# A twelve-stage perceiver on one core: weights, constants and first contexts loaded in the normalisation ahead of their stage

## The reference

```python
# L0x, L3x: cross attention of 16 heads, own Wq, Wk, Wv, Wo (L3x masked)
# L1x: the same with 16 heads of 64, a layer-normed context and clipped exponentials
# L2x: cross attention without weights: queries x, keys and values the context
# L0a linear attention, L1a retention, L2a softmax attention with normed heads, L3a gated recurrence
# L0f experts mixed per position, L1f routed experts (top 2 of 8), L2f one of 8 matrices per position,
# L3f SwiGLU with int8-like weights scaled by 1/127
```

## Time and profile before

| | us |
|---|---|
| median of 3 runs | 3187.68 (3183.82 to 3192.27) |
| the profiled execution | 3196.44 |
| its span | 3194.8 |
| TensorE busy | 2603.5 (81%) |
| VectorE busy | 1769.5 (55%) |
| ScalarE busy | 1363.4 (43%) |
| GpSimd busy | 563.6 (18%) |

### The profile page before, as it was taken

One profiled execution on the slowest core, in us unless ns is written; L12 is line 12 of the kernel. 1 busy time (PEld: TensorE's weight loads), 2 busy tenths in 40 slices (PEclk: granted clock), 3 DMA queues, 4 the chain that ended last, 5 costly groups with the idle time before them and its releaser, 6 DMA issues. The chain is left out here.

```text
span 3194.8 us, 84173 instructions
## 1 busy us (share of the span) xinstructions
PE 2603.5 (81%) x36049; PEld 2160.8 (68%) x36049; DVE 1769.5 (55%) x3318; ACT 1363.4 (43%) x3367; POOL 563.6 (18%) x717
## 2 busy tenths in 40 slices
PE   5999677999947999999977629928986756999868
PEld 4888454777745888888865529926764635888547
DVE  4777573566645444444345415636755855666553
ACT  3777322445522344343322214406753333666332
POOL 1111001111002211111112030043322412222000
PEclk8999898999978999999986559968987787999989
DMA  2110002110012000000000223223210001111000
GB/s 68 35 35 15 15 0 86 55 55 29 16 53 67 15 19 24 15 15 2 2 11 13 68 102 135 90 69 95 90 46 5 2 28 47 46 43 43 11 30 27
DMA packets 118713, 129.74 MB, mean 41 GB/s; under 512 B 10606, under 2 KB 109882, under 8 KB 118362
## 3 DMA queue, kind: packets, MB, share of 16 engines
q1 hardware_dynamic: 113882, 110.93, 11.2%
q0 software_dynamic: 4480, 13.64, 1.3%
...
## 5 line engine op out<-in xcount | busy, mean ns | idle before, releaser
L562 ACT ACTIVATE s_ca_probs<-s_ca_scores,s_ca_neg_max 128x256 f32<-128x256 f32 x768 | 353.2, 482 | 13.4 <-DVE s_ca_neg_max L606 10.2
L606 DVE TENSOR_REDUCE s_ca_neg_max<-s_ca_scores 128x4 f32<-128x1024 f32 x192 | 234.1, 1220 | 108.5 <-PE s_ca_scores L473 55.9
L485 PE MATMUL s_ca_probs_flipped<-identity,s_ca_probs 128*128 128x128 f32 x1536 | 212.5, 282 | 15.8 <-ACT s_ca_probs L562 9.8
L1003 DVE RECIPROCAL s_cc_inv_sums<-s_cc_sums 128x512 f32<-128x512 f32 x32 | 107.4, 3357 | 182.5 <-PE s_cc_out L871 182.5
L485 PEld LDWEIGHTS s_ca_probs_flipped<-identity,s_ca_probs 128*128 128x128 f32 x1536 | 167.2, 142 | 58.9 <-ACT s_ca_probs L562 26.6
L1665 DVE COPY s_mx_w_mixed<-s_mx_ps 128x512 f32<-128x512 f32 x256 | 163.6, 683 | 61.5 <-PE s_mx_ps L1512 45.1
L568 ACT COPY s_ca_probsT<-s_ca_probs_flipped 128x512 f32<-128x512 f32 x192 | 114.7, 597 | 173.1 <-PE s_ca_probs_flipped L485 173.1
L1620 ACT COPY s_mx_w_mixed<-s_mx_ps 128x512 f32<-128x512 f32 x256 | 137.4, 589 | 117.2 <-PE s_mx_ps L1499 97.6
L163 PE MATMUL s_ln_flip<-identity,s_ln_xn 128*128 128x128 f32 x352 | 64.3, 366 | 139.4 <-DVE s_ln_xn L145 139.2
L562 ACT ACTIVATION_READ_ACCUMULATOR s_ca_probs<-s_ca_scores,s_ca_neg_max 128x1 f32 x768 | 164.7, 214 | 0.0
L789 POOL TENSOR_TENSOR s_cc_probs_of_both<-s_cc_probsT 128x1024 f32<-128x1024 f32 x32 | 76.8, 2402 | 495.3 <-DVE s_cc_probsT L994 495.3
...
## 6 DMA issues: line engine op xcount, KB each, us to landing
...
```

Source lines behind the costliest of these rows:

```text
L485: last = nc.tensor.transpose(psT[:, 2 * a + c, :], PR[b % 2][:, 4 * n + a, c * P:(c + 1) * P], ident[:, :])
L562: last = nc.scalar.activation(PR[b % 2][:, p, :], psS[:, p // 2, (p % 2) * NKEY:(p % 2 + 1) * NKEY], ACT.Exp, bias=nmax[b % 2][:, p:p + 1] ...
L606: nc.vector.tensor_reduce(nmax[b % 2][:, 4 * n:4 * n + 4], psS[:, 2 * n:2 * n + 2, :].rearrange("p r (g k) -> p r g k", g=GR), AX_X, ALU.m ...
L1003: nc.vector.reciprocal(RD[:, :, :], psD[:, :, :]).then_inc(s_rd, 1)
```

## The change

Each block's weights become an object (`ProjectionWeights`, `CrossWeights`, `ClippedWeights`, `LinearWeights`, `GateWeights`, `PositionWeights`, `ValueWeights`, `RetentionWeights`, `HeadWeights`, `SoftmaxWeights`, `TileWeights`, `RecurrenceWeights`, `QuantisedWeights`) whose tensors and semaphores outlive the stage (`held`) and whose `load` is issued on SP in the normalisation ahead. Five have a `prepare` on POOL: splits of weights and of two contexts and zeroed values (L0x, L3x, in the query projection), splits of the four weight pieces and the normalising of the first rows (L1x, in the query projection, where DVE takes the statistics of the first rows and SP loads the pieces), the reorder (L0f, in the gate stage), zeroed and copied values (L2x, in the normalisation), and the scaling of the quantised weights (L3f, in the recurrence). The tile weights of L2f are loaded in the normalisation ahead of L2a, behind L2a's own, and the quantised weights of L3f in that ahead of L3a. `project_transposed` works in pieces of 128 weight columns and of one input chunk, with two input buffers in place of the whole input. `swiglu_quantised` does the same, is written out without a loop, and interleaves up and down. The bias matmuls of the cross attentions move behind the first key and value projections. L1f (routed experts) is not touched. The semaphores of the held objects are cleared once at the end, with one more barrier. The stages not shown below replace their loads by the object's fields.

```diff
+@contextmanager
+def held(nc, kept):
...
+        def sem(name):
+            s = nc.alloc_semaphore(unique(name))
+            kept.append(s)
+            return s
+
+        yield sb, sem
...
+class ProjectionWeights:
+
+    def __init__(self, sb, sem, w, bias, chunks):
+        self.w, self.bias = w, bias
+        self.W, self.B = sb("pj_w", [P, KC, chunks * P]), sb("pj_b", [P, chunks])
+        self.s_w, self.s_b = sem("pj_w_loaded"), sem("pj_bias_loaded")
+
+    def load(self, sp):
+        sp.dma_start(self.W[:, :, :], rows_to_sbuf(self.w)).then_inc(self.s_w, 16)
+        if self.bias is not None:
+            sp.dma_start(self.B[:, :], self.bias).then_inc(self.s_b, 16)
...
+    def prepare(self, pool):
+        for u in range(2):
+            pool.memset(self.V[u][:, :, :, :, :], 0.0).then_inc(self.s_set, 1)
+        if self.OWN:
+            pool.wait_ge(self.s_wkv, 16)
+            pool.tensor_copy(self.WH[:, :, :], self.W[:, :, :]).then_inc(self.s_wh, 1)
+            pool.wait_ge(self.s_wh, 1)
+            pool.tensor_tensor(self.WL[:, :, :], self.W[:, :, :], self.WH[:, :, :].bitcast(F32), ALU.subtract).then_inc(self.s_wl, 1)
+            for b in range(2):
+                pool.wait_ge(self.s_ct[b], 16)
+                pool.tensor_copy(self.CH[b][:, :, :], self.CT[b][:, :, :]).then_inc(self.s_ch, 1)
+                pool.wait_ge(self.s_ch, b + 1)
+                pool.tensor_tensor(self.CL[b][:, :, :], self.CT[b][:, :, :], self.CH[b][:, :, :].bitcast(F32),
+                                   ALU.subtract).then_inc(self.s_cl, 1)
+            pool.wait_ge(self.s_w, 96)
+            pool.tensor_copy(self.BVS[:, :, :], self.BV[:, :].unsqueeze(2).broadcast_to([P, KC, P])).then_inc(self.s_const, 1)
+        else:
+            pool.wait_ge(self.s_set, 2)
+            for b in range(2):
+                self.values(pool, b)
...
+    def load(self, sp):
+        sp.dma_start(self.rows_of(0), self.groups[0]).then_inc(self.s_in[0], 16)
+        sp.dma_start(self.COL[:, 0, :], self.ln_w).then_inc(self.s_col, 16)
+        sp.dma_start(self.COL[:, 1, :], self.ln_b).then_inc(self.s_col, 16)
+
+    def load_more(self, sp):
+        for n, (c, q) in enumerate(self.PIECES):
+            if n >= 2:
+                sp.wait_ge(self.s_wl, n - 1)
+            sp.dma_start(self.RAW[n % 2][:, :], self.wkv[c * P:(c + 1) * P, q * self.INNER:(q + 1) * self.INNER]).then_inc(self.s_raw[n % 2], 16)
+
+    def prepare(self, pool):
+        for n, (c, q) in enumerate(self.PIECES):
+            cols = slice(q * self.INNER, (q + 1) * self.INNER)
+            pool.wait_ge(self.s_raw[n % 2], 16 * (n // 2 + 1))
+            pool.tensor_copy(self.WH[:, c, cols], self.RAW[n % 2][:, :]).then_inc(self.s_wh, 1)
+            pool.wait_ge(self.s_wh, n + 1)
+            pool.tensor_tensor(self.WL[:, c, cols], self.RAW[n % 2][:, :], self.WH[:, c, cols].bitcast(F32), ALU.subtract).then_inc(self.s_wl, 1)
+        for b in range(self.GB):
+            self.normalise(pool, b)
...
+    def prepare(self, pool):
+        self.reorder1(pool, 0)
+        self.reorder2(pool, 0)
...
+    def prepare(self, pool):
+        for n, (src, dst) in enumerate(((self.WI[0], self.W[0]), (self.WI[1], self.W[1]), (self.WDI, self.WD))):
+            pool.wait_ge(self.s_w[n], 16)
+            pool.tensor_scalar(dst[:, :, :], src[:, :, :], 1.0 / 127.0, None, ALU.mult).then_inc(self.s_f, 1)
...
                 if affine:
                     for n, v in enumerate(affine):
                         sp.dma_start(col[:, n, :], v).then_inc(s_col, 16)
+                for weights in loads:
+                    weights.load(sp)
 
             @block.gpsimd
             def _(pool):
                 nc.gpsimd.memset(eps[:, :], EPS).then_inc(s_eps, 1)
+                if prepare:
+                    prepare(pool)
 
...
+            if aside is not None and isinstance(aside, ClippedWeights):
+                @block.sync
+                def _(sp):
+                    aside.load_more(sp)
+
+            if aside is not None:
+                @block.gpsimd
+                def _(pool):
+                    aside.prepare(pool)
 
             @block.scalar
             def _(act):
-                for t in range(NT):
-                    if t == 1:
-                        act.wait_ge(s_w, 16)
-                        nc.scalar.copy(WS[0][:, :, :], W[:, :, :]).then_inc(s_wh, 1)
-                    nc.scalar.copy(XS[0][:, :, t * TC:(t + 1) * TC], XNT[:, :, t * TC:(t + 1) * TC]).then_inc(s_xh, 1)
+                def high_weights(m):
+                    cols = slice(m * P, (m + 1) * P)
+                    nc.scalar.copy(WS[0][:, :, cols], W[:, :, cols]).then_inc(s_wh, 1)
+
+                def high_input(t):
+                    if t >= 2:
+                        act.wait_ge(s_mm, (t - 1) * chunks)
+                    for c in range(KC):
+                        nc.scalar.copy(XS[0][:, c, t % 2, :], XNT[:, c, t * TC:(t + 1) * TC]).then_inc(s_xh, 1)
+
+                act.wait_ge(s_w, 16)
+                high_weights(0)
+                high_input(0)
+                for m in range(1, chunks):
+                    high_weights(m)
+                high_input(1)
+                if isinstance(aside, ClippedWeights):
+                    aside.roots(act, 0)
+                for t in range(2, NT):
+                    high_input(t)
 
             @block.tensor
             def _(pe):
-                pe.wait_ge(s_wl, 1)
                 for n, (t, m) in enumerate(jobs):
-                    if m == 0:
-                        pe.wait_ge(s_xl, t + 1)
+                    if t == 0:
+                        pe.wait_ge(s_wl, m + 1)
                     if n >= 4:
                         pe.wait_ge(s_st, n - 3)
                     for c in range(KC):
+                        if m == 0:
+                            pe.wait_ge(s_xl, KC * t + c + 1)
                         last = three_passes(nc, out[n % 4][:, :], [v[:, c, m * P:(m + 1) * P] for v in WS],
-                                            [v[:, c, t * TC:(t + 1) * TC] for v in XS], c == 0, c == KC - 1)
+                                            [v[:, c, t % 2, :] for v in XS], c == 0, c == KC - 1)
                     last.then_inc(s_mm, 1)
 
             @block.vector
             def _(dve):
+                def low_weights(m):
+                    cols = slice(m * P, (m + 1) * P)
+                    dve.wait_ge(s_wh, m + 1)
+                    nc.vector.tensor_tensor(WS[1][:, :, cols], W[:, :, cols], WS[0][:, :, cols].bitcast(F32), ALU.subtract).then_inc(s_wl, 1)
+
                 def low_input(t):
-                    dve.wait_ge(s_xh, t + 1)
-                    cols = slice(t * TC, (t + 1) * TC)
-                    nc.vector.tensor_tensor(XS[1][:, :, cols], XNT[:, :, cols], XS[0][:, :, cols].bitcast(F32), ALU.subtract).then_inc(s_xl, 1)
-
+                    for c in range(KC):
+                        dve.wait_ge(s_xh, KC * t + c + 1)
+                        nc.vector.tensor_tensor(XS[1][:, c, t % 2, :], XNT[:, c, t * TC:(t + 1) * TC],
+                                                XS[0][:, c, t % 2, :].bitcast(F32), ALU.subtract).then_inc(s_xl, 1)
+
+                low_weights(0)
                 low_input(0)
-                dve.wait_ge(s_wh, 1)
-                nc.vector.tensor_tensor(WS[1][:, :, :], W[:, :, :], WS[0][:, :, :].bitcast(F32), ALU.subtract).then_inc(s_wl, 1)
+                for m in range(1, chunks):
+                    low_weights(m)
+                low_input(1)
                 if bias is not None:
                     dve.wait_ge(s_b, 16)
                 for n, (t, m) in enumerate(jobs):
-                    if m == 0 and t + 1 < NT:
-                        low_input(t + 1)
                     dve.wait_ge(s_mm, n + 1)
...
                 pe.wait_ge(s_set, 2)
                 if OWN:
+                    pe.wait_ge(s_wl, 1)
+                    project_keys(0)
+                    project_values(0)
+                    project_keys(1)
                     pe.wait_ge(s_const, 4)
                     for c in range(KC):
                         nc.tensor.matmul(psO[:, 0:DIM], BVS[:, c, :], WO[:, c, :], start=(c == 0), stop=False)
                     nc.tensor.matmul(psO[:, 0:DIM], ones[0:1, :], BO[:, :], start=False, stop=True).then_inc(s_bias, 1)
-                    pe.wait_ge(s_wl, 1)
-                    project_keys(0)
-                    project_values(0)
-                    project_keys(1)
                     pe.wait_ge(s_bb, 1)
...
-                pe.wait_ge(s_w, 64)
-                nc.tensor.matmul(psO[:, 0:4, :].rearrange("p m q -> p (m q)"), ones[0:1, :], BO[:, :], start=True, stop=True).then_inc(s_bias, 1)
                 flip(0)
                 flip(1)
-                pe.wait_ge(s_wl, len(PIECES))
+                pe.wait_ge(s_wl, len(held.PIECES))
                 for k in range(4):
                     keys(0, k)
+                pe.wait_ge(s_w, 32)
```

(38 more changed lines are left out.)

911 lines of the change are left out of this document (500 added, 411 removed).

## The result

The kernel now takes 3081.4 us in the median of four runs (3068.0 to 3086.2) against 3190.0 for the kernel before: a ratio of 0.9655, 95% interval 0.9621 to 0.969, faster. The forecast was 3068.5 with a range of 3044 to 3104. The profiled execution took 3079.7 us (span 3078.0) against 3196.4 (span 3194.8). Of the span 116.8 us are gone; the forecast for it was 119.2.

The account below looks back on a forecast made before the run. Stage starts waiting on loads, TensorE idle, were taken as fully on the path. Savings 55.9 + 21.0 + 19.5 + 12.8 + 4.0, less 1.0 and 1.0, plus clock's 8: 119.2, so 3187.7 becomes 3068.5 us; range 3044 to 3104.

Parts of the forecast that it names:

- The start stretches: Stage starts, first instruction to first matmul or scores: on the path in full; plain stages and values by token together 55.9 us.
- clipped attention's scores: Clipped cross attention's start, 33.3 us to first scores: first scores 13 to 14 us in, minus 19.5 us.
- the two own cross attentions: L0 and L3 cross attentions: first scores from 19.1 and 21.8 us to 10.1 and 9.8, together minus 21.0.
- The price of POOL: L0, L3 and L1 projections: DVE steps wait for POOL's instruction in progress, together minus 4.0 us; in the recurrence plus 1.0.
- the term for L1: L1's projection: two DVE statistics steps wait at 2.3 us, 4.7 of the 7.3 us gain lost, minus 2.6.
- the term of 1.0: Recurrence: three scalings on POOL meet DVE's first steps, plus 1.0 us, between 0 and 4.
- Values by token: Values by token stage: its load goes but the 6.92 us memset on POOL stays, so only minus 0.4 us.
- The clock: Some eight stage starts: matmuls beginning earlier skip part of the low-clock stretch, 8 us taken, between 0 and about 21.
- the port decides in three projections: L0, L3 and L1 projections: rival that the shared port gives 25 us back, 3094 us; chance 0.13.
- Another wait behind the removed one: Half of the stage starts: rival that another wait stands behind the removed load, 20 to 35 us missing, 3096; chance 0.10.
- The rival on the slower side: L0, L3, L1 projections: POOL's preparations hold stage ends, gain gone at 10.7 ns an element, 3212 us at 12; chance 0.03.
- The moved issues: Normalisations: DMA issues moved onto SP cost nothing, at most 2 us if more is held back.

Follow-up runs that it names:

- Late statistics: Changed kernel with DVE's statistics of the first context rows moved from behind the fifth to behind the seventeenth output of L1's query projection: ratio 0.9629, that stage 49.4 us.
- extra products: Against the kernel with six loads back, TensorE multiplies something nobody reads while waiting for loads: ratio 0.977; with half as many, 0.9753, six stages 645.2 us.

## Why the prediction was right, point by point

**The start stretches** were the right reading of the earlier trace rows: 125.5 us saved by the windows, where the forecast's terms, before POOL's price and the clock, give 120.3. The largest misses are small ones: clipped attention's scores came 11.9 us in, not 13.8, and the two own cross attentions' 9.2, not 10.1 and 9.8. They ran at the full clock, where the 8.0 us that the 10.1 was built on had run at 0.81. Putting six loads back lengthened the starts by 31.1 us and their stages by 31.5 (34.9 in the repeated run): such a stretch lies on the path in full. The other stages' loads were not put back one by one; for them the table stands alone.

**The price of POOL** had the mechanism right and the term for L1 too small. Two of the steps were let wait at 2.3 us, 4.7 in all; measured, four steps waited (0.7, 2.05, 0.8 and 2.0 us), TensorE paused 5.8 and then ran at the low clock for about 5 us, and 8.0 us were lost, more than the 7.4 saved at the start: the stage gained nothing where 2.6 were forecast. Late statistics brought 8.5 us. The 1.3 us taken for a POOL cast of 1024 was 1.04 to 1.06 undisturbed, and its subtraction 2.36 to 2.40 for 2.36; POOL never held a stage end. In the recurrence the term of 1.0 was 3.1 on the stage, by the run with the scalings on ACT, inside its bounds of 0 to 4.

The Trainium skill (SBUF — State Buffer, Who interferes with whom) says which pairs meet at the shared ports: a VectorE step with two SBUF inputs against a GpSimd one that reads SBUF, and a copy or scalar step in a two-port mode against any. The trace agrees in each case seen here: beside a memset 0.18 us for the step with two inputs and 6.12 for the one with one source; beside a subtraction 2.22 for two inputs; beside a cast 0.90 for one source; copies from PSUM unharmed. Which mode a step ran in, no trace shows. The rule beside the list of DVE's steps says that nearly each of them can wait; how many do is then a matter of when each one starts.

**Values by token** was a small term that failed, -0.4 forecast and +1.1 measured: TensorE did four tiles, then rested 3.71 us for the memset and lost the clock. The prediction had it that TensorE waits as before; it left out that an earlier start only lengthens that rest. That the memset decides was right, and shown: 15.3 us without the wait.

**The clock** as a gain of 8 us over eight starts is the step that did not hold as put. At the recurrence the time from TensorE's first matmul to DVE's first step fell by exactly the 2.6 us worked out. In L2's attention the clock came back 17 us into the stage instead of 24, and behind the first scores the stage took 205.0 us instead of 208.2. That repeats: in seven of the eight profiles with the early load the clock came back after 16.6 to 18.4 us and the stage took 206.1 to 207.5; in the eighth it came back after 41 and the stage took 217.0; in the three with the late load and no extra products it was 24 to 27.5 us and 214.1 to 216.6. Elsewhere no gain is clear of the scatter between executions with the same code in the stage (softmax 113.1 to 117.3 us, linear attention 111.0 to 114.3, position experts 389 to 397). That TensorE's rest in the gap costs the clock is borne out in the recurrence, and more weakly in the gates, where the extra products kept it or brought it back early; it is not shown as a pattern: with the loads back and TensorE kept busy, the six stages took 645.2 us against 641.4 and 644.8 without. Why an earlier start brings the clock back earlier in L2's attention stays open.

Part of the forecast's closeness is thus luck, errors against each other. The starts saved 5.2 us more than the forecast's terms. Behind the starts the stages lost 6.5 us in the profiles (125.5 less 119.0), where the clock's 8 us were to outweigh POOL's price. And by the medians the saving was 108.6, not 119.2.

**The rivals.** That the port decides in three projections was half true: it took all of L1's gain, 8 us, but in L0's and L3's projection 0.8 and 1.7 us at most. Another wait behind the removed one was right for values by token alone. The rival on the slower side needed POOL at 10.7 ns an element; its share in L0's projection, 4.4 thousand elements, lasted 11.5 us with two memsets (27.9 to 39.4), 2.6 ns each, and L1's 10 thousand took 20.6 busy us. The moved issues cost nothing where a cost was feared: the normalisation ahead of the gates takes 11.8 us in both kernels. The one that grew most is the kernel's first, from 14.4 to 15.2 us.
